# All rows for the first projections, and the middle tile's second projection in four quarters of the array

## What is computed

```python
rw = jax.nn.sigmoid(pooled @ Wr + br)
Wk = jnp.einsum('be,ecm->bcm', rw, Wpw)
h = jnp.einsum('bhwc,bcm->bhwm', x, Wk) + (rw @ bpw)[:, None, None, :]
h = jax.nn.relu(_bn(h, g1, b1, m1, v1))          # 24 -> 96 channels
h = _cond_dw(h, Wdw, bdw, rw)                    # 3x3 taps per channel
h = jax.nn.relu(_bn(h, g2, b2, m2, v2))
Wk2 = jnp.einsum('be,emf->bmf', rw, Wpwl)
h = jnp.einsum('bhwm,bmf->bhwf', h, Wk2) + (rw @ bpwl)[:, None, None, :]
h = _bn(h, g3, b3, m3, v3)                       # 96 -> 24 channels
return h + shortcut
```

## Time and profile before

| | |
|---|---|
| median of 3 runs | 2684.66 us (2683.72 to 2687.61) |
| profiled execution | 2684.42 us, span 2682.3 us |
| instructions | 49164, of them 19776 matmuls |
| busy: PE, DVE, ACT, POOL | 2305.7, 1948.2, 1678.5, 69.0 us |
| mean granted clock of TensorE | 0.88 of full speed |
| DMA | 29.56 MB, 11 GB/s in the mean |

### The profile page before, as it was taken

One profiled execution on the slowest core, in us unless ns is written; L12 is line 12 of the kernel. 1 busy time (PEld: TensorE's weight loads), 2 busy tenths in 40 slices (PEclk: granted clock), 3 DMA queues, 4 the chain that ended last, 5 costly groups with the idle time before them and its releaser, 6 DMA issues.

```text
span 2682.3 us, 49164 instructions
## 1 busy us (share of the span) xinstructions
PE 2305.7 (86%) x19776; PEld 1278.3 (48%) x19776; DVE 1948.2 (73%) x3879; ACT 1678.5 (63%) x2824; POOL 69.0 (3%) x130
## 2 busy tenths in 40 slices
PE   3776988999889997999889998899879998987765
PEld 2233434664336733555336743465335553563552
DVE  4884977788857896697948788587866989466243
ACT  3344457756667567766856667766766668657654
POOL 1000000000000000000000000000000000000000
PEclk9887979989879897899879898899887998978766
DMA  4001001000020002000020000100010000000000
GB/s 132 1 1 19 1 1 19 2 2 1 1 36 2 1 1 37 2 1 1 1 37 2 1 1 2 36 2 1 1 28 2 2 1 1 20 1 1 19 1 19
DMA packets 108593, 29.56 MB, mean 11 GB/s; under 512 B 104144, under 2 KB 104272, under 8 KB 107984
## 3 DMA queue, kind: packets, MB, share of 16 engines
q1 hardware_dynamic: 108368, 26.41, 4.9%
HBM read 16.77 MB, written 9.63 MB: 10 GB/s over the span
## 4 chain that ended last, share of the span: by engine, by line
PE 59%; DVE 20%; ACT 12%; issue 4%; SPq 3%; DMA 1%; ACTq 0%; DVEq 0%
PE P L720 12%; PE P L701 9%; DVE acc L1417 7%; PE P L765 6%; PE P L915 4%; PE P L737 4%; PE P L741 3%; PE P L928 3%; SPq L574 2%; PE P L956 2%; PE P L756 2%; DVE SQ L1558 2%; PE P L866 2%; PE P L779 2%; PE P L940 1%
## 5 line engine op out<-in xcount | busy, mean ns | idle before, releaser
L1417 DVE SCALAR_TENSOR_TENSOR acc<-H,Dm,acc 128x784 f32<-128x784 f32 x1024 | 991.3, 1028 | 86.7 <-ACT acc L1083 86.3
L701 PE MATMUL P<-T,Wk 48*128 48x448 f32 (+5 forms) x768 | 402.5, 626 | 40.4 <-ACT H L1076 19.9
L720 PE MATMUL P<-H,diag 64*64 64x392 f32 x4608 | 401.0, 498 | 5.8 <-DVE T L1433 5.7
L1076 ACT ACTIVATE H<-P,biasA 128x448 f32<-128x448 f32 (+1 forms) x384 | 235.7, 621 | 216.2 <-PE P L701 145.9
L720 PEld LDWEIGHTS P<-H,diag 64*64 64x64 f32 x4608 | 171.5, 134 | 215.0 <-issue 201.9
L765 PE MATMUL P<-T,pack_b 112*112 112x448 f32 x448 | 245.0, 637 | 21.3 <-ACT mid L1124 6.6
L701 PEld LDWEIGHTS P<-T,Wk 64*128 64x128 f32 (+2 forms) x768 | 128.1, 205 | 177.5 <-ACT H L1076 73.8
L1106 ACT ACTIVATE acc<-P,biasT 128x392 f32<-128x392 f32 x128 | 69.1, 584 | 181.2 <-PE P L720 181.2
L1083 ACT ACTIVATE acc<-H,Dm 128x784 f32<-128x784 f32 x128 | 121.4, 949 | 49.5 <-PE P L741 47.2
L737 PE MATMUL P<-acc,Wk 64*112 64x392 f32 x256 | 118.7, 587 | 28.7 <-ACT acc L1112 28.6
L1433 DVE SCALAR_TENSOR_TENSOR T<-P,bias,T 112x392 f32<-112x392 f32 x128 | 78.6, 623 | 80.3 <-PE P L741 79.1
(11 more groups left out here) (192 smaller groups left out, 3800.7 us busy)
## 6 DMA issues: line engine op xcount, KB each, us to landing
xin<-in_x SPq DMA_DIRECT2D x224, 42.0 KB, 2.2
out_y<-arena SPq DMA_DIRECT2D x8, 1176.0 KB, 6.0
pack_b<-in_pack_b SPq DMA_DIRECT2D x1, 3820.5 KB, 17.4
arena<-in_pack_s SPq DMA_DIRECT2D x1, 1548.0 KB, 8.5
pack_a<-in_pack_a SPq DMA_DIRECT2D x1, 1084.0 KB, 5.3
pack_i<-in_pack_i SPq DMA_DIRECT2D x1, 320.0 KB, 3.1
arena<-in_pack_k SPq DMA_DIRECT2D x1, 192.0 KB, 3.2
```

The source lines that it names most:

```text
L701: pe.matmul(conv_rows(slice(0, 128), HB[(NP * s + e) % len(HB)], n), Wk1[rows, 128 * j:128 * (j + 1)], image_rows(T[q % 3][rows, :], a, n) ...
L720: last = pe.matmul(conv_rows(slice(64 * h, 64 * (h + 1)), CVB + r, HH), diag[64 * r:64 * (r + 1), tap, :], H1[64 * r:64 * (r + 1), slot(s, ...
L1076: act.activation(H1[:, slot(s, j), o:o + n, 1:1 + HW], conv_rows(slice(0, 128), HB[(NP * s + e) % len(HB)], n), ACT.Relu, bias=biasA[:, j, ...
L1417: ins = ve.scalar_tensor_tensor(a, H1[:, slot(s, j), r:r + SR, c:c + HW], Dm[:, j, tap:tap + 1], a, ALU.mult, ALU.add)
```

## The change

In `hidden` all first projections read the 112 rows of `T` and of the weights `Wk1`, which are zero in the rows of other images (`maskI`). In `conv_out` the products of tile 1 are cut by output rows: channel half 0 belongs to image 1 and writes rows 0 to 63 only, half 1 to image 2 and rows 64 to 111 only. They become four products of 64 x 64 and 64 x 48, each a quarter of the array of its own, in place of two sums of two. A `yield` stands behind them, and only the products of tiles 0 and 2 wait for h2_ready. `TURNS` is new for `tensor`, `scalar` and `vector`, with 192 steps of d in place of 128 for `tensor`. A line or two of it stands in the diff. As the strings are two lines longer, L701, L720, L741 and L1106 of before are L702, L721, L743 and L1108 of after, and L737 stays.

```diff
-                        rows = {0: slice(0, 64), TJ: slice(0, R), 2: slice(64, R)}[j]
-                        pe.matmul(conv_rows(slice(0, 128), HB[(NP * s + e) % len(HB)], n), Wk1[rows, 128 * j:128 * (j + 1)],
-                                  image_rows(T[q % 3][rows, :], a, n), start=True, stop=True).then_inc(h1_psum.sem, 1)
+                        pe.matmul(conv_rows(slice(0, 128), HB[(NP * s + e) % len(HB)], n), Wk1[:, 128 * j:128 * (j + 1)],
+                                  image_rows(T[q % 3], a, n), start=True, stop=True).then_inc(h1_psum.sem, 1)
...
                 yield
                 pe.wait_ge(t2_ready.sem, t2_ready.at(q, 2 * (L * NS + s + 1)))
-                pe.wait_ge(h2_ready.sem, h2_ready.at(q, L * NV + 2 * (s + 1)))
-                for r in range(2):
+                for r, out_rows in enumerate((slice(0, 64), slice(64, R))):
                     for h in range(2):
                         rows = slice(64 * h, 64 * (h + 1))
                         w = Wk2p[rows, TJ * RC:TJ * RC + R] if r == h else Wk2t[rows, :]
-                        pe.matmul(conv_rows(slice(0, R), CVB + h, HH), w,
-                                  image_rows(acc[rows, (NT * s + TJ) % N2, :], HH * r, HH), start=(r == 0), stop=False)
+                        pe.matmul(conv_rows(out_rows, CVB + h, HH), w[:, out_rows],
+                                  image_rows(acc[rows, (NT * s + TJ) % N2, :], HH * r, HH), start=True, stop=False)
+                yield
+                pe.wait_ge(h2_ready.sem, h2_ready.at(q, L * NV + 2 * (s + 1)))
                 for h in range(2):
                     for j, out_rows, w in ((0, slice(0, 64), Wk2p[:, 0:64]), (2, slice(64, R), Wk2[:, 2, 2 * CH:RC])):
...
-        "m1 c28 d2 c15 d2 c14 d1 c1 d1 c9 d2 c25 d1 c1 d1 c23 d2 c16 d1 c1 d1 c1 d2 m1 c1 m1 c1 m2 c1 m4 c17 "
+        "m1 c27 d2 c18 d1 c1 d1 c18 d1 c1 d1 c2 d2 c23 d1 c1 d1 c18 d2 c15 d1 c1 d1 c9 d2 m1 c1 m1 c1 m2 c1 "
```

More of the change, by code:

```diff
@@ L84 @@
     "gpsimd": (
-        "d7 b2 c11 m1 c10 m1 c5 b1 c4 b1 c3 m1 c3 b1 c4 b1 c2 m1 c4 b1 c4 b1 c2 m1 c4 b1 c4 b1 c2 m1 c4 b1 c4 "
-        "b1 c2 m1 c4 b1 c3 b1 c1 m1 b2 "
+        "d7 b2 c11 m1 c12 m1 c3 b1 c4 b1 c2 m1 c4 b1 c4 b1 c2 m1 c4 b1 c4 b1 c2 m1 c4 b1 c4 b1 c2 m1 c4 b1 c4 "
+        "b1 c2 m1 c4 b1 c4 b1 m1 b2 "
     ),
     "tensor": (
[44 rows of a table removed]
[46 rows of a table added]
     ),
     "scalar": (
[37 rows of a table removed]
[37 rows of a table added]
     ),
     "vector": (
[24 rows of a table removed]
[24 rows of a table added]
     ),
```

## The result

The changed kernel takes 2542.2 us (2536.1 to 2547.1) against 2684.4 us: a ratio of 0.9467, with an interval of 0.9441 to 0.9493. The direction was right; the size was not.

A forecast was written before the change was run, and what follows sets the result against it. PE was taken to bound the kernel for nearly 2000 us, DVE and ACT close behind. Savings of 45 + 26 + 6 = 77 us less 15 taken back gave 2684 - 62 = 2622, rounded to 2620 us; range 2575 to 2665.

The forecast's parts named there:

- The step of its own: In conv_out, tile 1's products wait for t2_ready alone, filling PE's idle time ahead of L737: 6 us saved.
- changes of array tile: All-rows first projections cut PE's tile changes from 1128 to 891: 39 us of PE time, 26 us on the path.
- the middle tile's projection: L737 as four quarter products takes 0.81 us for 1.51, 64 times: 45 us saved, all on the path.
- The rule on weight loads: Skill's rule that loads overlap only across differing row groups: all-rows projections would lose about 100 us; rejected on the 112-row L701.
- What the others take back: DVE and ACT become last more often as PE gets faster: a fifth of the savings taken off, -15 us.
- Rival 3: PE stands at the new first half in conv_out, waiting for ACT: gain gone or slower, up to 2710 us; chance 0.05.
- rival 2: DVE and ACT take back most and idle PE loses its clock: 2640 to 2679 us; chance 0.13.
- Rival 1: All 84 us of PE savings count, some at half clock, and the order removes waits: 2570 to 2590 us; chance 0.13.
- the signs: What the profile after should show: product forms and lengths, PE busy about 2220 us, short L1108 waits, clock near 0.88.
- the forms: Profile after should show 64x64 and 64x48 forms of L737 and no 64x128 form of L702.
- the short waits for L1108: PE's waits for L1108 ahead of L737 should stay under 20 us in all.

The follow-up runs named there:

- e3: Kernel before with only L737's products cut into four quarters, in the old order and one step: 2655.7 us, ratio 0.9882.
- e6: Changed kernel with the first projections on 64, 112 and 48 rows again: 2621.0 us, ratio 0.9754.
- e9: Changed kernel with a one-column 64 x 64 product ahead of each tile 0 first projection, adding 182 changes of tile: 2563.7 us, ratio 0.9537.
- e10: Changed kernel with first projections reading 80, 88 and 112 rows, all in a tile of 128 rows: 2549.0 us, ratio 0.9480.
- e12: Changed kernel with six probes of 50 PE products appended, varying rows, columns and waiting, executed once: 3038 us in total, which means nothing as a time.
- e5: Changed kernel with the new step left empty, tile 1's products directly ahead of L743 and waiting for h2_ready too: 2577.0 us, ratio 0.9599.
- e13: Kernel before with the new order but old products, the new step left empty and L737 directly ahead of L743: 2683.2 us, ratio 0.9991.
- e4: Changed kernel with both product edits undone, keeping its new order and two steps of conv_out: 2610.6 us, ratio 0.9708.
- e1: Kernel before with both product edits (112-row projections, quarters) in the old order and one step: 2609.4 us, ratio 0.9705.
- e8: Changed kernel with the four quarter products issued twice, 42 us more PE work: 2551.3 us, ratio 0.9502.

## Why the prediction was wrong, by its steps

Two terms of the sum failed: "The step of its own", 6 us for what measured 35 to 76, and the worth of the changes of array tile, 26 us for what measured 51 to 79. The third, the middle tile's projection, was too high.

- **The middle tile's projection.** Its price on PE was right (0.80 us for 0.81). Its worth, "all of it on the path", was not: 32 us in the old order, 8 in the new, against 45. In e3 the clock stayed at 0.88, and DVE's share of the chain rose to 27%. The reason given, that L737's share of the chain, 107 us, is above its 97 us of work, was too thin: 4% is a rounded figure and means 94 to 121 us.
- **Changes of array tile.** The price of one change was right. The step that failed is "on the path lies about what L701 has there", 26 us: the rows were worth 51 us in the old order and 79 in the new. What was missing is the clock. I had put the work at half clock into the range as a factor on the work saved, and didn't ask whether the edit would change how much of the time is at that level. The lower level's 644 us became 494. That the tile of 64 rows is what kept the clock down in the kernel is inferred from e6, e9, e10 and e12.
- **The rule on weight loads.** It was rejected on a row, and rightly: the all-rows projection takes 0.75 us in the changed kernel too, with neighbours of its shape. "No longer than 2 x 448 columns" doesn't show it, though: at 2.4 GHz 0.76 us are 1824 clocks, four for each of 448 columns. What shows it is the shorter form: on 392 columns, all rows and like neighbours, the projection takes 0.675 us (median of 29 in the changed kernel) against 0.768 on 448 (median of 82). One of the 29:

```profile
891.55 0.82 PE L702 MATMUL P<-T,Wk 112*128 112x392 f32 x2
892.21 0.92 PE L767 MATMUL P<-T,pack_b 112*112 112x448 f32 x2
```

  That is nearly in proportion to the columns and leaves no room for two exposed loads of 0.2 us.
- **The step of its own.** "In each of them at most the 0.81 us that move ahead of the wait are won": this is the term that was mis-sized most, 6 us against 35 with the new products (e5) and 73 to 76 with the old ones (e13 against e4). I counted only the 20 places where PE stood idle ahead of L737. But after h2_ready every second projection still had L737 ahead of L741, whether PE had waited or not, and DVE (79.1 us) and ACT (47.2 us) waited for the end of L741. Those rows were in the profile of before and weren't used. Work that stands between a signal and a result delays whoever waits for the result, and its cost is seen there. What else the new order does was left to the range; with the new products it is worth 28 us more (e5 against e1).
- **What the others take back.** The direction was right, -15 us: DVE's share of the chain rose from 20 to 32%, and added work on PE now costs a fifth to over half of its length (e8, e9). It acted on the quarters, not on the other two.
- **The rivals.** Rival 3 didn't happen: L737 waited for 6.5 us in all. In rival 2 the clock was to fall; it rose. Rival 1 named the right side and, in a clause each, the half clock and the waits that the new order removes; but it gave them 10 to 30 us beyond PE's 84, where the gain is 58 beyond.

Of the signs, the forms, the 0.8 and 0.75 us and the short waits for L1108 came as written; PE's busy time (2173.5 us for 2220) and the clock (0.903 for 0.88) didn't. The parts don't add up exactly, and how the 142 us divide between clock and waits can't be read from any run: the clock follows what PE does, and both move together.

## What to carry to other kernels

When an edit moves work ahead of a signal, sum the waits of all engines for the last instruction behind that signal, not only the idle time ahead of the moved one. Where the clock is at its lower level for part of the span, ask of each edit what it does to that share; a product on few rows may be cheaper in a tile of all rows, even with zeros in the weights. And price an order together with the steps and products that it places: without the early half the new order was worth nothing with the old products, and 28 us with the new ones.

## What the runs showed of the hardware

- In probes (one execution) of one float32 product of 448 columns at a time, 64 rows in a 64 x 128 or 64 x 64 tile stood at 1.2 GHz, 80 and 112 rows in a tile of 128 rows at 2.4 GHz.
- A change of array tile costs about 0.09 us at each side of it, at 2.4 GHz (0.75, 0.84 and 0.94 us for L765), and 182 more of them left the clock at 0.902 to 0.912 (e9).
- More work on PE can cost little: twice the quarters, 42 us, cost 9 to 16 us, with the clock at 0.910 to 0.912 after 0.903 to 0.911.
- Executions of one kernel differ by up to 1.2%, and their mean clock with them: 2667.6 us at 0.887 and 2698.9 at 0.874 in e13, 2598.0 at 0.897 and 2618.8 at 0.886 in e1.
